# Conditioned residual on one core: the weight table is loaded in 2048 runs of 512 B in place of 128 runs of 8 KB

## The reference

```python
# x: (64, 128, 2048) float32;  itok_B_0_15: (64,) int32 in 0..15;  weights: (16, 128, 128) float32
W = weights[condition]
x = x + jnp.einsum('bct,bcd->bdt', x, W)
```

## Time and profile before

| | |
|---|---|
| median of 3 runs | 320.15 us (319.94 to 320.36) |
| the profiled execution | 320.04 us, span 318.3 us |
| PE busy | 246.5 us (77%), 512 matmuls |
| DVE busy | 146.8 us (46%) |
| POOL busy | 18.9 us (6%) |
| moved by DMA | 135.29 MB in 5187 packets, mean 425 GB/s |
| queue 1 (SP's), queue 10 (ACT's) | 50.0% and 48.9% of the 16 DMA engines' time |

### The profile page before, as it was taken

One profiled execution on the slowest core, in us unless ns is written; L12 is line 12 of the kernel. 1 busy time (PEld: TensorE's weight loads), 2 busy tenths in 40 slices (PEclk: granted clock), 3 DMA queues, 4 the chain that ended last, 5 costly groups with the idle time before them and its releaser, 6 DMA issues.

```text
span 318.3 us, 1351 instructions
## 1 busy us (share of the span) xinstructions
PE 246.5 (77%) x512; PEld 104.6 (33%) x512; DVE 146.8 (46%) x65; POOL 18.9 (6%) x69
## 2 busy tenths in 40 slices
PE   0099999991996979779398895939979596796960
PEld 0044444440442424334143342414424242342420
DVE  0026766762252553735237362641626556055460
POOL 0000000000010000001000010000000001000000
PEclk9999999998796998999779799996979999598996
DMA  8999999999999999999999999999999999999997
GB/s 329 416 441 457 371 424 457 397 461 399 457 424 432 449 408 461 412 445 432 424 453 404 457 424 432 445 412 461 399 457 424 432 449 408 461 395 461 420 411 298
DMA packets 5187, 135.29 MB, mean 425 GB/s; under 512 B 578, under 2 KB 578, under 8 KB 578
## 3 DMA queue, kind: packets, MB, share of 16 engines
q1 hardware_dynamic: 2448, 68.16, 50.0%
q10 hardware_dynamic: 2738, 67.11, 48.9%
HBM read 68.16 MB, written 67.11 MB: 425 GB/s over the span
## 4 chain that ended last, share of the span: by engine, by line
DMA 61%; PE 33%; DVE 3%; issue 0%; SPq 0%
PE product L92 33%; DMA out<-x_ring 32%; DMA x_ring<-x 30%; DVE x_ring L108 3%; SPq L58 0%
## 5 line engine op out<-in xcount | busy, mean ns | idle before, releaser
L92 PE MATMUL product<-x_ring,chosen_weights 128*128 128x512 f32 x512 | 246.5, 644 | 61.4 <-DMA x_ring<-x 61.4
L108 DVE TENSOR_TENSOR x_ring<-product,x_ring 128x2048 f32<-128x2048 f32 x64 | 146.7, 2291 | 161.4 <-PE product L92 161.4
L92 PEld LDWEIGHTS product<-x_ring,chosen_weights 128*128 128x128 f32 x512 | 104.6, 207 | 202.4 <-issue 122.7
L80 POOL COPY chosen_weights<-weight_table 128x128 f32 x64 | 18.7, 293 | 284.6 <-DVE x_ring L108 277.7
L102 DVE TENSOR_SCALAR state_row<-condition_row 1x64 int32<-1x64 int32 x1 | 0.2, 182 | 2.0 <-DMA condition_row<-condition 2.0
L137 POOL MEMSET const-float32-0.0<- 128x1 f32 x1 | 0.1, 98 | 0.1
L137 POOL MEMSET const-bfloat16-1.0<- 128x1 bf16 x1 | 0.1, 101 | 0.0
L137 POOL MEMSET const-uint8-127<- 128x1 uint8 x1 | 0.1, 101 | 0.0
L137 POOL MEMSET const-float32-1.0<- 128x1 f32 x1 | 0.1, 98 | 0.0
L137 POOL BASE_LOAD x1 | 0.0, 12 | 0.1
## 6 DMA issues: line engine op xcount, KB each, us to landing
x_ring<-x SPq DMA_DIRECT2D x16, 4096.0 KB, 26.7
out<-x_ring ACTq DMA_DIRECT2D x15, 4096.0 KB, 31.3
out<-x_ring ACTq DMA_DIRECT2D x4, 1024.0 KB, 9.1
weight_table<-weights SPq DMA_DIRECT2D x1, 1024.0 KB, 4.9
condition_row<-condition ACTq DMA_DIRECT2D x1, 0.2 KB
```

Of the source, the lines that this page charges most:

```text
L80: pool.tensor_copy(chosen_weights[b][:, :], weight_table[:, bass.ds(state[b] * features, features)]).then_inc(weights_chosen[b], 1)
L92: last = pe.matmul(product[:, b % psum_slots, m * BANK_COLUMNS:(m + 1) * BANK_COLUMNS], chosen_weights[b][:, :], x_ring[:, bass.ds(b * tim ...
L108: dve.tensor_tensor(tile, product[:, b % psum_slots, :], tile, AluOpType.add).then_inc(sum_done[b], 1)
```

## The change

The host no longer transposes the weights. Their array in HBM is now (16 states, 128 channels, 128 features), as it is given, in place of (channels, states, features). A channel's 16 rows of 128 float32, which were one run of 8 KB, are now 16 runs of 512 B, 64 KB apart. The DMA reads them with a rearranged view of the source and writes them to the same places of `weight_table` as before: 2048 runs of 512 B in one DMA, still the first on SP's queue. No instruction is added, removed or moved on any engine; on SP the shape of this one DMA goes from 128x2048 to 128x16x128.

```diff
-    _, states, features = weights.shape
+    states, _, features = weights.shape
...
-            sp.dma_start(weight_table[:, :], weights.rearrange("c s d -> c (s d)")
-                          ).then_inc(table_loaded, 16)
+            sp.dma_start(weight_table[:, :].rearrange("c (s d) -> c s d", s=states),
+                         weights.rearrange("s c d -> c s d")).then_inc(table_loaded, 16)
...
-        "weights": np.ascontiguousarray(np.asarray(L0_cond_weights).transpose(1, 0, 2)),
+        "weights": np.ascontiguousarray(L0_cond_weights),
```

## The result

| | time, us | runs | against before, 95% interval |
|---|---|---|---|
| before | 320.18 (319.94 to 320.36) | 6 | |
| changed | 321.15 (320.96 to 321.96) | 6 | 1.0034 (1.0023 to 1.0045) |
| changed, in a second comparison (after_again) | 321.52 (320.83 to 322.27) | 9 | 1.0039 (1.0027 to 1.0051) |

The change costs 0.97 us in the first comparison and 1.25 us in the second, where 0.85 us was forecast (321.0 us). The size was right. The trace shows that the way to it was right only in part.

The account below looks back on a forecast made before the run. The prediction took the DMA engines as the bound: the table's 128 runs on each engine take 3.33 us in place of 2.48 us, 0.85 us more, so 320.15 + 0.85 = 321.0 us. The range was 320.3 to 323.0 us.

Parts of the forecast that it names:

- The DMA engines bound the kernel, and what is added ahead of x arrives at the end: DMA engines: 98.9% taken, nothing idle from 5.35 to 313.00 us, so time added before the first load reaches the end.
- The whole 0.85 us arrives: End of the kernel: all 0.85 us added to the table's load shows there, since nothing is caught up later.
- PE starts 0.85 us later, and so does the end: PE's first matmul: at 16.3 us in place of 15.44 us, with every later store and load late by the same 0.85 us.
- Bytes at 27.2 B per ns and 5.6 to 8.5 ns fixed for a packet: Price of a table packet on a DMA engine: 512 B take 18.8 ns for bytes, 24.4 to 27.3 ns in all, 26 ns taken.
- 2048 packets for the table: Table load on SP's queue: each 512 B run is its own packet, 7,107 packets in all in place of 5,187.
- the prediction's lower bound of 24.4 ns: Table load: a 512 B run priced with the small packet's fixed part, 3.12 us for 128, 0.64 us more.
- The forecast of 3.33 us for 128 runs: Table load on each of 16 engines: 128 x 26 ns in place of 8 x 0.310 = 2.48 us, 0.85 us more.
- SP's issue is one instruction for one, under 0.6 us: SP's issue of the table: still one instruction, now of three dimensions; it took 372 ns and should stay under 0.6 us.
- slower pieces: Rival, table load: pieces made or read slower than 26 ns an engine, end 2.8 us more, 322.95 us; chance 0.17.
- Absorbed: Rival, table load: a packet's fixed part is hidden or under 5 ns, up to 0.6 us more, 320.5 us in the middle; chance 0.31.
- The rule of the Trainium skill: Table load: 3 fixed cycles a packet give 22.4 ns for 512 B, 0.4 us more, which would count as no change.

Follow-up runs that it names:

- twice_8k: The kernel before with the table loaded a second time into a spare buffer, in runs of 8 KB: 322.80 us, 2.4 us over before.
- x_first_512: The changed kernel with the table's DMA issued behind the first load of x instead of ahead of it: 320.58 us, 1.0012 of before.
- twice_512: The changed kernel with the table loaded a second time into a buffer nobody reads: 324.36 us, 4.0 us over the kernel before.
- runs_256: The changed kernel with each matrix cut in two halves, 4096 runs of 256 B, 32 KB apart: 322.46 us, 1.0072 of the kernel before.
- x_first_8k: The kernel before with the table's DMA issued behind the first load of x: 320.05 us, 0.9996 of the kernel before.
- near_runs: The changed kernel with its 2048 runs of 512 B only 1 KB apart in HBM, not 64 KB: 321.24 us, 1.0029 of the kernel before.
- two_queues: The changed kernel with the table in two DMAs, states 0 to 7 on SP's queue, 8 to 15 on ACT's: 340.30 us, 1.0623 of before.
- act_512: The changed kernel with the whole table DMA on ACT's queue behind the indices: 346.51 us, 1.0819 of the kernel before.
- runs_1k: The changed kernel with two states side by side, 1024 runs of 1 KB, 128 KB apart: 320.14 us, 0.9999 of the kernel before.

## Why the prediction was right or wrong

- *The DMA engines bound the kernel, and what is added ahead of x arrives at the end.* Right to first order: twice_8k's 2.5 us of packets came out as 2.4 us. Not to the last half microsecond. The prediction read the share of 1.00 from 5.35 to 313.00 us as no free DMA time. But a share is time and not bytes: from 36 to 42 us the kernel before moves 350 GB/s, where it moves 434 GB/s from 42 to 300 us, since packets of x stall. The changed kernel lost 0.3 us less there, x_first_512 and twice_512 0.7 us less; runs_256, x_first_8k and twice_8k lost as much. "The whole 0.85 us arrives" was too strict.
- *PE starts 0.85 us later, and so does the end.* PE starts 1.73 us later (17.17 against 15.44 us). It waits for the slowest of the 16 engines, so its start says more than what the engines are behind on average, 1.3 us at 36 us.
- *Bytes at 27.2 B per ns and 5.6 to 8.5 ns fixed for a packet.* Right as the time of a packet where each run is one: 27.0 ns for 512 B, 46.5 ns for 1 KB (37.6 + 8.9). The pace of 512 B packets is faster, 23.7 ns, as they overlap.
- *2048 packets for the table.* Wrong. In the changed kernel four runs share a packet, 85.6 ns beside packets of x, which is 21.4 ns a run, below the prediction's lower bound of 24.4 ns. The forecast of 3.33 us for 128 runs was met only as an average, 3.70 against 2.87 us with the slow first packets on both sides, since the packets stretch to 119 ns later on.
- *SP's issue is one instruction for one, under 0.6 us.* Wrong. It takes 0.84 us, behind an added shape instruction, and the table's first packet starts after 2.4 us in place of 1.8 us. I had this only as a mechanism of the rival "slower pieces", with the issue time growing by the piece to 5.95 us. It goes with this form of the instruction: 0.64 us in near_runs with as many runs, 0.83 us in runs_256 with twice as many. Its weight is small: x_first_512, where it is covered, is 1.2 us behind at 36 us, and the changed kernel 1.3 us. In the kernel before the first six packets started early but took 1.12 us each, and the other engines' started after 2.4 us too.
- *Slower pieces, 2.8 us.* The size didn't happen, the mechanism did in part (119 ns, and 76% busy engines in near_runs). The scattered reads don't pace them: two_queues read at the same jumps at 666 runs a us. What paces the packets of four, the making of the pieces or something else, stays open.
- *Absorbed.* As a time true for 1 KB runs, not for 512 B: the interval of the changed kernel begins at 0.7 us.
- *The rule of the Trainium skill* ("DMA: Bandwidth & Descriptors", section "Why small descriptors are slow (HBM only)"), 3 cycles for a packet, gives (64 + 3) / 0.85 = 78.8 ns for a packet of 2 KB as an estimate from the page; 85.6 ns were measured in act_512. For a lone run of 512 B it gave 22.4 ns; the pace of near_runs was 23.7 ns and the time of a packet 27.0 ns. The trace is above it both times. What the prediction drew from it, no measurable change, missed the slow first microsecond and the 119 ns.

So the right number was in part luck, from two errors of opposite sign. The table put the engines 1.3 us behind and not 0.85 us, and some 0.3 us of it were given back where the prediction had nothing.

## What to carry to other kernels

Where the DMA engines are full from the first load to the last store, price every transfer ahead of the first load in engine time. A share of 1.00 of the DMA engines doesn't say that they move at their full rate: compare the GB/s of the stages too, since a stretch with stalled packets can take up half a microsecond. Here runs of 1 KB cost nothing; at 512 B ask how the DMA is issued and packed before counting packets. And don't put a transfer of many small packets that something waits for on a second queue beside one with 32 KB packets: here it got one small packet for each large one, 144 for 144.

## What had not been expected of the hardware

- Two queues alternate by packets and not by bytes: 144 to 144 in 10 us at 2 KB against 32 KB. It made a table of 1 MB land after 44.4 us, and the kernel 26 us slower.
- Four runs of 512 B or of 256 B went as one packet in some forms of the DMA and not in others: near_runs, with runs 1 KB apart, and two_queues, with 8 states in place of 16 at the same jumps, had one run a packet. The first issues with packed runs took 0.81 to 0.84 us and had a MOVE_SHAPE before them.
- Short packets overlap: 27.0 ns each, but one in 23.7 ns on each engine (near_runs).
- Loads of x stalled for some 0.7 us on each engine from 36 to 42 us (350 GB/s), and less or not at all in five versions (changed, near_runs, runs_1k, x_first_512, twice_512).
- The packed packets took 85.6 ns beside packets of x, and up to 119 ns when all 16 engines moved nothing else.
